# Reordering the first two tiles of a LoRA kernel, with the A factors stored r-major

## The reference, cut to what matters

```python
def L0(x, condition, weights):                # x [64, 32, 512]
    return einsum('bct,bcd->bdt', x, weights[condition])
def L1(x, adapter_mapping, W, b, lora_As, lora_Bs):
    base_out = einsum('bti,oi->bto', x, W) + b            # W [512, 512]
    A, Bm = lora_As[adapter_mapping], lora_Bs[adapter_mapping]   # [512, 16], [16, 512]
    lora_h = einsum('bti,bir->btr', x, A)
    return base_out + einsum('btr,bro->bto', lora_h, Bm) * 2
x = x + L0(x, itok_B_0_15, L0_cond_weights)
x = x + L1(x, itok_B_0_23, L1_cond_W, L1_cond_b, L1_cond_lora_As, L1_cond_lora_Bs)
```

## Time and profile before

| what | value |
|---|---|
| median of 3 runs | 84.74 us (84.66 to 84.76) |
| the profiled execution | 84.83 us, of which 83.0 us from the first to the last instruction |
| busy share of the span | PE 94%, PEld 86%, DVE 72%, ACT 63%, POOL 40% |
| granted TensorE clock | 1.0 of full speed in the whole span |
| chain that ended last | PE 85%, DMA 6%, ACT queue 3%, ACT 2%, DVE 1% |

### The profile page before, as it was taken

How to read it: one execution, slowest core, us unless ns; L and a number is a source line. 1 busy time by engine, 2 the same in 40 slices (tenths; PEclk the granted TensorE clock), 3 DMA queues, 4 the chain that set the end, 5 groups by cost and what they waited for, 6 DMA issues and landing times.

```text
span 83.0 us, 2012 instructions
## 1 busy us (share of the span) xinstructions
PE 78.5 (94%) x524; PEld 71.2 (86%) x524; DVE 60.1 (72%) x158; ACT 52.4 (63%) x180; POOL 33.5 (40%) x75
## 2 busy tenths in 40 slices
PE   4999599999999999999999999999999999999970
PEld 2376498899999999999999999999999999999950
DVE  2049595877879787777878787978777777869560
ACT  1555758866666675958666666667685867665520
POOL 6108843744443517080715344352608071304300
PEclk9999999999999999999999999999999999999999
DMA  2899899998476766877668778667774626130334
GB/s 24 279 349 317 202 253 216 355 252 247 142 233 197 255 197 241 198 230 196 183 205 200 210 190 241 173 238 184 236 179 155 167 91 175 30 118 0 126 126 126
DMA packets 16141, 16.07 MB, mean 193 GB/s; under 512 B 10241, under 2 KB 10626, under 8 KB 16130
## 3 DMA queue, kind: packets, MB, share of 16 engines
q1 hardware_dynamic: 14016, 11.67, 46.9%
q0 software_dynamic: 1248, 4.06, 18.6%
q10 hardware_dynamic: 866, 0.21, 1.1%
HBM read 11.74 MB, written 4.19 MB: 192 GB/s over the span
## 4 chain that ended last, share of the span: by engine, by line
PE 85%; DMA 6%; ACTq 3%; ACT 2%; DVE 1%; issue 1%; DVEq 0%
PE z_ps L565 58%; PE z_ps L602 9%; DMA a_raw<-in_lora_a 6%; PE y_ps L617 4%; PE y_ps L615 4%; PE y_ps L613 4%; PE ht_ps L589 2%; ACTq L326 1%; PE ht_ps L652 1%; PE z_ps L597 1%; DVE y_sb L552 1%; ACT L320 1%; ACTq L316 1%; ACT a_sb L391 0%; ACTq L317 0%
## 5 line engine op out<-in xcount | busy, mean ns | idle before, releaser
L565 PE MATMUL z_ps<-wa,x_hi 128*128 128x288 f32 (+2 forms) x240 | 50.1, 301 | 0.0
L565 PEld LDWEIGHTS z_ps<-wa,x_hi 128*128 128x128 f32 x240 | 38.0, 188 | 1.8 <-issue 0.5
L565 PE MATMUL z_ps<-wa,x_lo 128*128 128x288 f32 (+2 forms) x120 | 35.3, 295 | 0.0
L565 PEld LDWEIGHTS z_ps<-wa,x_lo 128*128 128x128 f32 x120 | 22.6, 188 | 0.0
L303 POOL CAST m_hi<-m_raw 128x128 fp32r<-128x128 f32 x16 | 4.8, 301 | 35.3 <-ACT m_raw L340 35.3
L294 POOL DMA_INDIRECT b_raw<-in_lora_b,b_index_slot x16 | 16.8, 1048 | 4.4 <-POOL b_index_slot L292 4.4
L384 ACT CAST z_hi<-z_ps 128x256 fp32r<-128x256 f32 x31 | 10.1, 376 | 10.2 <-PE z_ps L602 10.1
L487 DVE TENSOR_TENSOR z_lo<-z_ps,z_hi 128x256 fp32r<-128x256 f32 x31 | 11.8, 420 | 6.3 <-ACT z_hi L384 6.3
L340 ACT COPY m_raw<-w_raw 32x32 f32 x64 | 13.8, 216 | 1.8 <-DVE w_raw L519 0.9
L446 DVE TENSOR_TENSOR x_lo<-x_raw,x_hi 128x512 fp32r<-128x512 f32 x14 | 9.7, 690 | 3.7 <-ACT x_hi L352 3.7
L467 DVE TENSOR_TENSOR b_lo<-b_raw,b_hi 128x512 fp32r<-128x512 f32 x15 | 10.4, 691 | 0.5
(11 more groups left out here) (58 smaller groups left out, 76.7 us busy)
## 6 DMA issues: line engine op xcount, KB each, us to landing
out<-y_sb SPq DMA_DIRECT2D x15, 256.0 KB, 2.4
x_raw<-in_xt SPq DMA_DIRECT2D x14, 256.0 KB, 3.2
a_raw<-in_lora_a SPq DMA_DIRECT2D x60, 32.0 KB, 2.9
first_sb<-in_first SPq DMA_DIRECT2D x2, 384.0 KB, 3.9
first_sb<-in_first SPq DMA_DIRECT2D x3, 256.0 KB, 4.8
b_raw<-in_lora_b,b_index_slot POOLq DMA_INDIRECT x16, 4.0
bias_sb<-in_bias SPq DMA_DIRECT2D x1, 256.0 KB, 4.3
a_raw<-in_lora_a ACTq DMA_DIRECT2D x4, 32.0 KB
```

The source lines that it names most:

```text
L565: done = nc.tensor.matmul(target, (x_lo if lo_x else x_hi)[s][:, k, :], moving(lo_w), start=first and not lo_x and not lo_w, stop=last and ...
```

## The change

A is laid out on the host as j, r, k instead of j, k, r: the four chunks of one rank stand side by side in a partition. A chunk of it is then a pattern with a single step of four words, which the weight load of tile 0's h takes as it is, and the copy `a0_sb` goes. The reads of A by `round_a` and `rest_a` of every tile step by four words too; before, they read runs of 16 words.

Tile 1 takes the first half of W without A (256 columns) and the second half with all of A (320 columns). Its first half starts before tile 0's h, part by part, and h of tile 0 stands inside it. `lora(0)` moves behind two chunks of the second half. ACT and DVE handle the last chunk of W before A of tile 1. `load_a(3)` waits for tile 0's h. For later tiles the wait for both halves of z of tile u-2 is split in two.

```diff
-        a_raw = [sb(f"a_raw{s}", [P, J, KC, R], F32) for s in range(NA)]
-        a0_sb = sb("a0_sb", [P, KC, JR], F32)
+        a_raw = [sb(f"a_raw{s}", [P, J, R, KC], F32) for s in range(NA)]
...
+        def a0_chunk(k):
+            return a_raw[0][:, :, :, k:k + 1].rearrange("p j r a -> p (j r a)")
...
         def a_half(u, half):
-            return a_raw[u % NA][:, half * HJ:(half + 1) * HJ, :, :].rearrange("p j k r -> p k j r")
+            return a_raw[u % NA][:, half * HJ:(half + 1) * HJ, :, :].rearrange("p j r k -> p k j r")
+        WITH_A = {1: 1, LAST: 0}
...
                 if u == NA:
-                    sp.wait_ge(a0_ready, 1)
+                    sp.wait_ge(main_done, 1)
...
             round_x1(0)
-            act.wait_ge(a_loaded[0], 16 * J)
-            act.copy(a0_sb[:, :, :].rearrange("p k (j r) -> p k j r", j=J),
-                     a_raw[0][:, :, :, :].rearrange("p j k r -> p k j r")).then_inc(a0_ready, 1)
             round_x1(1)
+            round_w(KC - 1)
             round_a(1)
-            round_w(KC - 1)
...
             rest_x1(1)
+            rest_w(3)
             rest_a(1)
-            rest_w(3)
...
             def wait_main(u):
-                pe.wait_ge(x_ready, u + (u > 1))
-                pe.wait_ge(a_ready, 2 * u - (u == 1))
-                if u >= 2:
-                    pe.wait_ge(z_ready, 2 * (u - 1))
+                pe.wait_ge(x_ready, u + 1)
+                pe.wait_ge(a_ready, 2 * u)
+                pe.wait_ge(z_ready, 2 * (u - 1) - 1)
...
+            def first_h():
+                pe.wait_ge(a_loaded[0], 16 * J)
+                for k in range(KC):
+                    last = nc.tensor.matmul(ht_ps[0:JR, 0:P], a0_chunk(k), x0_chunk(k), start=k == 0,
+                                            stop=k == KC - 1, skip_group_check=True)
+                last.then_inc(main_done, 1)
...
+            pe.wait_ge(w_ready, 3)
+            half_chunk(1, 2, 0, (HH, HL))
+            pe.wait_ge(x_ready, 2)
+            half_chunk(1, 2, 0, (LH,))
+            first_h()
...
+            half_chunk(1, 0, 1)
+            half_chunk(1, 1, 1)
+            lora(0, 0)
+            lora(0, 1)
+            half_chunk(1, 2, 1)
+            half_chunk(1, 3, 1).then_inc(main_done, 1)
```

More of the change, by code:

```diff
@@ L26, in lora_residual_program @@
     C, S0, _ = w0.shape
-    SLOTS, _, _, R = lora_a.shape
+    SLOTS, _, R, _ = lora_a.shape
     T = KC * P
@@ L139, in lora_residual_program @@
         a_ready = sem("a_ready")
-        a0_ready = sem("a0_ready")
         b_hi_ready = sem("b_hi_ready")
@@ L179, in a_half @@
         def a_half(u, half):
-            return a_raw[u % NA][:, half * HJ:(half + 1) * HJ, :, :].rearrange("p j k r -> p k j r")
+            return a_raw[u % NA][:, half * HJ:(half + 1) * HJ, :, :].rearrange("p j r k -> p k j r")
+        WITH_A = {1: 1, LAST: 0}
         def a_place(u, half, lo):
-            row, at = (0, A_AT[1] + half * AC) if u == LAST else (half, A_AT[u % 2])
+            row, at = (WITH_A[u], A_AT[1] + half * AC) if u in WITH_A else (half, A_AT[u % 2])
             return wa[:, :, lo, row, at:at + AC].rearrange("p k (j r) -> p k j r", j=HJ)
         def h_of(u):
-            if u == LAST:
-                return z_ps[1][:, 0, HALF:HALF + 2 * AC].rearrange("p (a j r) -> p a j r", a=2, j=HJ)
+            if u in WITH_A:
+                return z_ps[1][:, WITH_A[u], HALF:HALF + 2 * AC].rearrange("p (a j r) -> p a j r", a=2, j=HJ)
             at = H_PS[u % 2]
@@ L230, in load_a @@
                     slot = sp.snap(adapters[j], min_val=0, max_val=SLOTS - 1)
-                    sp.dma_start(a_raw[u % NA][:, j:j + 1, :, :].rearrange("p j k r -> p j (k r)"),
-                                 lora_a[bass.ds(slot, 1)].rearrange("s p k r -> p s (k r)")
+                    sp.dma_start(a_raw[u % NA][:, j:j + 1, :, :].rearrange("p j r k -> p j (r k)"),
+                                 lora_a[bass.ds(slot, 1)].rearrange("s p r k -> p s (r k)")
                                  ).then_inc(a1_half_loaded[j // HJ] if u == 1 else a_loaded[u % NA], 16)
@@ L325, in _ @@
                 slot = act.snap(adapters0[j], min_val=0, max_val=SLOTS - 1)
-                act.dma_start(a_raw[0][:, j:j + 1, :, :].rearrange("p j k r -> p j (k r)"),
-                              lora_a[bass.ds(slot, 1)].rearrange("s p k r -> p s (k r)")
+                act.dma_start(a_raw[0][:, j:j + 1, :, :].rearrange("p j r k -> p j (r k)"),
+                              lora_a[bass.ds(slot, 1)].rearrange("s p r k -> p s (r k)")
                               ).then_inc(a_loaded[0], 16)
@@ L560, in _, with products, half_chunk @@
                                  start=True, stop=True)
[L562 to L566, removed]
+            HH, HL, LH = (0, 0), (0, 1), (1, 0)
+            def products(u, k, target, moving, parts=(HH, HL, LH)):
+                for part in parts:
+                    done = nc.tensor.matmul(target, (x_hi, x_lo)[part[0]][u % 2][:, k, :], moving(part[1]),
+                                            start=k == 0 and part == HH, stop=k == KC - 1 and part == parts[-1],
                                             skip_group_check=True)
                 return done
+            def half_chunk(u, k, half, parts=(HH, HL, LH)):
+                n = HALF + 2 * AC if half == WITH_A[u] else HALF
+                return products(u, k, z_ps[1][:, half, 0:n], lambda lo: wa[:, k, lo, half, AC:AC + n], parts)
             def main_chunk(u, k, half):
                 s = u % 2
[L572 to L577, removed]
+                if k == 0 and half == 1:
+                    pe.wait_ge(z_ready, 2 * (u - 1))
                 return products(u, k, z_ps[s][:, half, 0:NW],
-                                lambda lo: wa[:, k, lo, half, MOV[s]:MOV[s] + NW], k == 0, k == KC - 1)
+                                lambda lo: wa[:, k, lo, half, MOV[s]:MOV[s] + NW])
             def wait_main(u):
-                pe.wait_ge(x_ready, u + (u > 1))
-                pe.wait_ge(a_ready, 2 * u - (u == 1))
-                if u >= 2:
-                    pe.wait_ge(z_ready, 2 * (u - 1))
+                pe.wait_ge(x_ready, u + 1)
+                pe.wait_ge(a_ready, 2 * u)
+                pe.wait_ge(z_ready, 2 * (u - 1) - 1)
             def transpose_h(u):
@@ L649, in _ @@
                 first_chunk(k)
[L650 to L656, removed]
+            def first_h():
[4 more added lines that the diff above has]
+                last.then_inc(main_done, 1)
+            pe.wait_ge(x_hi_ready, 1)
+            for k in range(2):
+                pe.wait_ge(w_ready, k + 1)
+                half_chunk(1, k, 0, (HH, HL))
+            pe.wait_ge(x_ready, 1)
+            for k in range(2):
+                half_chunk(1, k, 0, (LH,))
+            pe.wait_ge(x_hi_ready, 2)
+            pe.wait_ge(w_ready, 3)
[3 more added lines that the diff above has]
+            first_h()
+            pe.wait_ge(w_hi_ready, KC)
+            half_chunk(1, 3, 0, (HH, LH))
+            pe.wait_ge(w_ready, KC)
+            half_chunk(1, 3, 0, (HL,))
+            pe.wait_ge(a_ready, 2)
+            half_chunk(1, 0, 1)
[4 more added lines that the diff above has]
+            half_chunk(1, 3, 1).then_inc(main_done, 1)
+            for u in range(2, LAST):
                 wait_main(u)
                 main_chunk(u, 0, 0)
[L660 to L664, removed]
+                main_chunk(u, 0, 1)
+                mix(u - 2)
+                transpose_h(u - 1)
+                main_chunk(u, 1, 0)
                 main_chunk(u, 1, 1)
@@ L673, in last_chunk @@
             def last_chunk(k, half):
-                n = (HALF + 2 * AC, HALF)[half]
-                return products(LAST, k, z_ps[1][:, half, 0:n], lambda lo: wa[:, k, lo, half, AC:AC + n],
-                                k == 0, k == KC - 1)
+                if k == 0 and half == 1:
+                    pe.wait_ge(z_ready, 2 * (LAST - 1))
+                return half_chunk(LAST, k, half)
             wait_main(LAST)
@@ L729 @@
         "bias": _np.broadcast_to(_np.asarray(inputs["L1_cond_b"]), (P, T)),
-        "lora_a": lora_a.reshape(-1, KC, P, R).transpose(0, 2, 1, 3),
+        "lora_a": lora_a.reshape(-1, KC, P, R).transpose(0, 2, 3, 1),
         "lora_b": _np.asarray(inputs["L1_cond_lora_Bs"]),
```

## The result

The changed kernel takes 87.25 us (87.16 to 88.09), the kernel before 84.75 us (84.66 to 84.77) on the same chip: a ratio of 1.0317, with an interval of 1.0277 to 1.0358. Forecast were 87.1 us and a range of 85.2 to 88.9. The profiled execution took 87.26 us, with a span of 85.5.

What follows compares the result with a forecast made beforehand. The prediction took PE as the bound, with a chain through ACT and DVE without slack; 84.83 - 0.5 (start) + 2.86 (single-word reads) = 87.2 us, or 87.1 against the median, range 85.2 to 88.9.

Steps and rivals of the forecast that it cites:

- The mechanism: In every later tile, single-word reads lengthen DVE's two rests of A, delaying the mask and `lora`: 0.22 us per tile.
- No slack: In later tiles, the chain through ACT and DVE to the mask and `lora` has no slack worth counting.
- the longer casts on ACT stay hidden: `round_a` on ACT finishes before DVE needs it, so 110 ns more for each cast still fit.
- The price: Single-word reads cost DVE 110 ns per rest of A, two per tile, 13 tiles: 2.86 us.
- The lower of the two estimates: From ACT's 0.7 ns per run, 128 runs of one word would cost 88 ns.
- The start: Filling PE's 0.88 us idle time ahead of tile 0's h brings tile 2 to 14.40; gain taken as 0.5 us.
- The 0.17 us taken off for the late load of tile 3's A: At the start, `load_a(3)` waits for tile 0's h, lands near 15.9 and gives back 0.1 to 0.2 us.
- The switch: On PE, changing between plain float32 and fp32r loses 0.19 us; the change adds two such switches around h.
- The term 0.5: The gain in us taken for the new order at the start, with ends 0.67 and about -0.2.
- Free words: Rival: single words cost DVE nothing, so only the start counts: 84.2 us, chance 0.12.
- A doubled load of h: Rival: words free, but h's stepped weight load delays `lora(0)` by up to 0.88 us: 84.9 to 85.0, chance 0.06.
- Slack of 0.1 us: Rival: DVE can lose 0.1 us per tile before PE notices: 85.8 us, counted inside the 0.82 for costly single words.

Runs made afterwards that it cites:

- the layout alone: The kernel before with only A laid out rank-major, keeping the copy of tile 0's A and the old order: 87.51 us, ratio 1.0327.
- mask first: The changed kernel with DVE's mask for `lora(u-1)` moved ahead of the rests of A of tile u+1: 84.24 us, ratio 0.9938.
- every second word: The kernel before with a pad word behind each word of A, so reads step by two words: 85.64 us, ratio 1.0085.
- the third of the last profiles: The changed kernel with DVE's mask moved ahead of the rests of A, profiled once more in one execution: 84.1 us.
- order alone: The changed kernel with A of tiles 1 to 15 in the old layout and tile 0's A rank-major in its own buffer: 84.71 us, ratio 0.9976.

## Why the prediction was right, and where it was not

**The mechanism was right.** Reads of single words make the rests longer, the mask is late, and PE waits at `lora` of each tile: the layout alone shows the loss, mask first takes it away with the price left in. "No slack" held too. That the longer casts on ACT stay hidden was right: they lasted 127 ns more, and mask first lost nothing by them.

**The price was over-stated.** 110 ns were taken, 92 measured. Twice 92 would be 0.184 per tile, 0.174 came, and 13 tiles make 2.26 instead of 2.86: 0.6 less. The lower of the two estimates, 88 ns from ACT's runs, was nearly the size on DVE; but a run's start is not its cause. The Trainium skill's figure ("Vector Engine (DVE) Microarchitecture Reference", "Measured stream behaviour on trn2"), 1.73 ns per column, agrees with 1.035 + 0.72 = 1.76 here. Its condition, runs of two or more adjacent words, does not: every second word took 286 ns. The note on cachelines in the Trainium skill's "SBUF — State Buffer" ("Door 1: The DMA port swizzle") wants two hits in each 16-byte line, which all three layouts agree with; that four fp32 are free does not hold here.

**The start failed at one step:** tile 0's chunks end at 8.50, and tile 1 can start at about 8.54. That end was taken from an execution in which the clock rose early, as if it were fixed. In the profile after, the last chunk starts at 8.84, so its successor was due at 9.06, 0.52 us after that start; and half of tile 1's x, rounded by 9.08, moved the effective start to 9.24, 0.70 late in all. Behind that the working held: the nine matmuls took 1.09 where 1.06 was forecast, and h with its switches 1.35 where 1.31 was the sum. `lora(0)` came at an effective 13.10 instead of 12.33 and tile 2 at 15.26 instead of 14.40, after a wait that was 0.09 us longer than the one foreseen there. The 0.17 us taken off for the late load of tile 3's A did not show, since nothing waited for it. So the start lost 0.18 us in that execution instead of gaining 0.5.

**The switch had the right size and the wrong name.** The prediction puts 0.19 us on a change between plain float32 and fp32r. Into and out of h and `lora(0)` it measured 0.19 to 0.20 again. But tile 0's chunks are plain float32 and tile 1 is fp32r, and that change is free. In the third of the last profiles the chunks' row ends at 8.76, so its last matmul, 0.38 long, starts at 8.38 and the next is due at 8.60; tile 1's row lasts 0.83 where four such matmuls, 0.12 apart and 0.285 long, last 0.645, so it starts effectively at 8.41 + 0.185 = 8.60. The transpose of h is plain float32 as well and stands between fp32r matmuls in every tile; in the profile before, nothing is lost there either (a transpose takes 0.11 us, and the row behind it 0.43 without a wait):

```profile
25.52 0.27 PE L589 MATMUL ht_ps<-ident,h_split 128*128 128x128 f32 x1
25.54 0.52 PE L565 MATMUL z_ps<-wa,x_hi 128*128 128x288 f32 x2
```

What the costly places share is the shape of the weights, `128*64` for h and `64*128` for `lora(0)`, against `128*128` on either side. That the shape is the cause fits all of these rows, but no run changes it alone.

With the earlier doubling, in the third of the last profiles, tile 2 starts at 14.59 (effective) against 15.07 before, a gain of 0.48. The term 0.5 is thus what the order brings in a good execution; the medians and the ratios say 0.1 to 0.2 (order alone) and 0.3 to 0.5 (with mask first).

So the sum by measured terms is 84.83 + 2.26 + 0.18 = 87.27, and 87.26 was measured. The forecast of 87.2 came as near as that by luck: two errors, -0.6 and +0.7, cancel.

**The rivals.** Free words: refuted by the rests at 376 ns. A doubled load of h: its eight weight loads did become longer, first before, then after (ns min/median/max):

```profile
L652 PEld LDWEIGHTS ht_ps<-first_sb,a_sb x8: 132/137/137, 9.4 to 10.1; 128*64 128x64 f32 x8
```

```profile
L657 PEld LDWEIGHTS ht_ps<-first_sb,a_raw x8: 194/209/217, 10.4 to 11.2; 128*64 128x64 f32 x8
```

72 ns more each would be 0.58 if nothing hid them; the stretch of h came out 0.04 longer than the sum, so the matmuls hide nearly all. Slack of 0.1 us: refuted by 4.468, 4.484 and 4.658 us per tile.

**What stays open.** What sets the moment at which PE's clock rises. In six profiles of the old order it lay between 3.8 and 5.4 us, in seven of the new between 5.6 and 7.1, although PE works back to back from 1.07 in all and has the same instructions up to there. The two groups do not overlap. If the order made no difference, thirteen draws would fall apart like that, old before new, in 1 case of 1716 (the ways to pick 6 of 13), so the moment seems to go with the program, within which it still varies by over 1 us; how the order could act on it no run shows. Why the load of tile 1's x came late in the profile after is open too.

## What to carry to other kernels

Before an operand's layout is changed for one reader, price the read for every other reader, and look whether one of them stands in a chain without slack: here the copy saved once cost 2 x 92 ns in 13 tiles. On a side engine, put the short instruction that the busy engine waits for ahead of the long ones that are wanted later; that was free here, worth about 0.3 us even without the change (0.9954), and with the new order gave the lowest median (0.9918). A start term read off one execution should carry the spread of that stretch, since an idle wait that is filled no longer hides it.

## What the runs showed of the hardware

- A float32 read on DVE of 128 columns takes 284 ns in runs of 16 words, 285 in pairs eight words apart, 286 for every second word and 376 for every fourth; on ACT 299, 317, 305 and 426. Words two apart still share 16 bytes, words four apart do not; that the 16 bytes are the reason, and not any step over two words, would take a step of three words, which no run has.
- A 64-column float32 weight load takes 209 ns instead of 137 at a step of four words.
- PE's matmuls at the start run at half their later pace until 3.8 to 7.1 us. The first entry of full clock in the trace starts at that moment; the views read 1.00 ahead of it because there is no entry.
- A change between plain float32 and fp32r with `128*128` weights on both sides costs nothing; into and out of weights of `128*64` or `64*128` PE loses 0.19 to 0.20 us.
